# Layer 3 attention: the loads of a tile split by batch around the row transfers, the statistics two quads later, and one maximum over two neighbouring banks

## The reference

```
qh = q.reshape(B, h, dq, Lq)      # B 64, h 8, dq 8, Lq 256
kh = k.reshape(B, h, dq, Lk)      # Lk 256
qk = jnp.einsum('bhdq,bhdl->bhql', qh, kh) * scale
sm = jax.nn.softmax(qk, axis=-1)
ret = jnp.einsum('bhql,bhdl->bhdq', sm, vh)
return gamma * ret                # added to x
```

## Time and profile before

| | |
|---|---|
| median of 3 runs | 2188.28 us (2182.26 to 2192.83) |
| the profiled execution | 2183.03 us |
| its span, first to last instruction | 2181.2 us |
| layer 3 attention, first scores to last read | about 1419 to 1826 us of the span |
| PE busy, whole span | 1794.5 us (82%) |
| DVE busy, whole span | 1546.7 us (71%) |
| mean granted clock of PE | 0.919 |

### The profile page before, as it was taken

The page is one execution under the profiler, slowest core; times in us unless marked ns, Lnnn a source line. Parts: engine busy times, 40 slices in busy tenths (PEclk is TensorE's granted clock), DMA queues, the critical chain, the costliest instruction groups (busy, mean ns, idle before and its releaser), DMA issues. The chain is left out here.

```text
span 2181.2 us, 43555 instructions
## 1 busy us (share of the span) xinstructions
PE 1794.5 (82%) x14590; PEld 1355.5 (62%) x14590; DVE 1546.7 (71%) x3825; ACT 982.8 (45%) x2422; POOL 893.5 (41%) x1043
## 2 busy tenths in 40 slices
PE   6989846299796688988988789779888886989993
PEld 5879712188565577777777678744444442557772
DVE  7975741278649789889889666588888894654446
ACT  3743231035233445545544333347877785533330
POOL 3410016534238466666666520013443443643330
PEclk9989955699899799999999899979999998999996
DMA  7821036520214000000000211026777763433337
GB/s 227 295 81 59 11 98 184 160 73 6 71 34 127 1 0 0 0 0 0 0 0 1 59 30 31 1 54 140 157 140 146 145 137 92 122 108 100 108 105 246
DMA packets 150753, 182.46 MB, mean 84 GB/s; under 512 B 40193, under 2 KB 132593, under 8 KB 146481
## 3 DMA queue, kind: packets, MB, share of 16 engines
q1 hardware_dynamic: 140769, 158.05, 27.9%
q0 software_dynamic: 9808, 22.23, 3.4%
HBM read 121.78 MB, written 56.79 MB: 82 GB/s over the span
## 5 line engine op out<-in xcount | busy, mean ns | idle before, releaser
L2885 DVE TENSOR_REDUCE mx<-bank 128x2 f32<-128x512 f32 x512 | 315.8, 680 | 25.5 <-PE bank L2764 24.9
L2857 ACT ACTIVATE e<-bank 128x512 f32<-128x512 f32 x512 | 280.4, 598 | 90.7 <-PE bank L2786 86.2
L1914 POOL TENSOR_TENSOR q_l<-q_l,rot_l 64x512 f32<-64x512 f32 x128 | 162.3, 1268 | 129.6 <-DVE rot_l L2112 129.6
L2801 PE MATMUL bank<-e,val 128*32 128x256 f32 x2048 | 166.0, 396 | 8.9 <-ACT nd L2852 8.3
L2786 PEld LDWEIGHTS bank<-q,k 64*128 64x128 f32 x1024 | 78.6, 189 | 135.8 <-ACT e L2857 79.5
L2786 PE MATMUL bank<-q,k 64*128 64x256 f32 x1024 | 131.3, 335 | 26.2 <-DMA q<-rows 19.8
L2764 PE MATMUL bank<-k,q 62*128 62x256 f32 x1024 | 112.5, 299 | 23.7 <-DVE mx L2885 19.9
L1946 PE MATMUL bank<-qcT,wq_abs 96*128 96x128 f32 x1024 | 126.0, 283 | 0.0
L1946 PEld LDWEIGHTS bank<-qcT,wq_abs 96*128 96x128 f32 x1024 | 120.2, 196 | 2.6
L3072 POOL DMA_INDIRECT y<-y,y_row x71 | 69.0, 972 | 125.4 <-DVE y L3347 121.2
L1971 PE MATMUL bank<-wvo,rd_l 128*128 128x256 f32 x512 | 116.2, 380 | 0.0
(11 more groups left out here) (445 smaller groups left out, 4688.3 us busy)
## 6 DMA issues: line engine op xcount, KB each, us to landing
k<-k_parts SPq DMA_DIRECT2D x128, 128.0 KB, 5.2
q<-q_parts SPq DMA_DIRECT2D x64, 256.0 KB, 4.3
got<-rows SPq DMA_DIRECT2D x71, 129.0 KB, 2.1
k_parts<-k_parts_a SPq DMA_DIRECT2D x64, 128.0 KB, 3.3
moe_rows<-zero_a SPq DMA_DIRECT2D x16, 512.0 KB
w<-in_e0w SPq DMA_DIRECT2D x16, 512.0 KB, 3.7
q_parts<-parts SPq DMA_DIRECT2D x64, 128.0 KB, 2.7
rec<-rec_rows SPq DMA_DIRECT2D x64, 128.0 KB, 2.5
```

Source lines behind the costliest of these rows:

```text
L1914: nc.gpsimd.tensor_tensor(q[64:P, j, four(m), :], q[64:P, j, four(m), :], rot[64:P, j, four(m), :], ALU.add).then_inc(s["rope_added"], 1)
L2801: last = nc.tensor.matmul(readout[32 * g:32 * g + 32, side], val[:, a.n % 2, g, i, lt, :], e[:, slot(i, r), lt, :], start=(i == 0 and lt = ...
L2857: nc.scalar.activation(e[:, slot(i, r), :, :].rearrange("p k n -> p (k n)"), scoresT(i, r)[:, :], ACT.Exp).then_inc(s["exp_ready"], 1)
L2885: v.tensor_reduce(mx[:, a.n, r % 2, 0, at:at + 2], scores(r)[:, :].rearrange("p (a n) -> p a n", a=2), AX.X, ALU.max, negate=True).then_in ...
```

## The change

The change has three parts. The first is the order of SP's queue. `load` is cut by batch. Before, SP's `tile(a)` ended with all six loads of tile a+4; now `tile(a)` begins with the three loads of batch 0 of tile a+3, then comes `gather`, then `lay_rows`, then `store_inverse`, and only then the three loads of batch 1 and the values of tile a+3, `store` and `load_inverse`. The wait of the load for the freed buffer is the same (`turned_ready` of the last unit of tile a-1). The second is one reduction on DVE over two neighbouring banks in the place of two; for this the eight bank tensors become one tensor `banks` of which `bank[k]` is a slice. The third is where DVE does its small work: `norm` after pair 0 of quad 0, `invert` after pair 1 of quad 0 (before in quad 1), and `stats` after quad 2 (before after quad 1). PE, ACT and POOL keep their code.

```
-            def load(a):
-                sp.wait_ge(s[stored[a.n % 2]], 32 * (uses(a) + 1))
-                settle(sp, s["sp_passed"])
-                for b, base in enumerate(BASE3):
-                    q_rows = batch_rows(c.q_parts, a.t, b).unsqueeze(1)
...
+            def load(a, b):
+                if b == 0:
+                    sp.wait_ge(s["turned_ready"], unit_ready(a.t - BUF, 3, 3))
+                    sp.wait_ge(s[stored[a.n % 2]], 32 * (uses(a) + 1))
+                    settle(sp, s["sp_passed"])
+                base, q_rows = BASE3[b], batch_rows(c.q_parts, a.t, b).unsqueeze(1)
...
+            def load_values(a):
                 if a.exists(-BUF):
                     sp.wait_ge(s["val_ready"], tile_ready(a.t) - BUF)
...
             def tile(a):
+                loading = a.exists(-1) and a.exists(BUF - 1)
+                if loading:
+                    load(a.to(BUF - 1), 0)
+                if a.exists(-1):
+                    gather(a.to(-1))
                 if a.exists(1):
                     lay_rows(a.to(1))
                 if a.exists(-2):
                     store_inverse(a.to(-2))
+                if loading:
+                    load(a.to(BUF - 1), 1)
+                    load_values(a.to(BUF - 1))
                 if a.exists(AHEAD):
                     store(a.to(AHEAD))
-                if a.exists(-1):
-                    gather(a.to(-1))
                 if a.exists(-2):
                     load_inverse(a.to(-2))
-                if a.exists(BUF):
-                    sp.wait_ge(s["turned_ready"], unit_ready(a.t, 3, 3))
-                    settle(sp, s["sp_passed"])
-                    load(a.to(BUF))
...
-            def maxima(a, i, r):
-                if i == 0 and r == 0:
+            def maxima(a, i, p):
+                if i == 0 and p == 0:
...
-                dve.wait_ge(s["scores_ready"], unit_ready(a.t, i, r))
-                at = 2 * (QU * (r // 2) + i)
-                v.tensor_reduce(mx[:, a.n, r % 2, 0, at:at + 2], scores(r)[:, :].rearrange("p (a n) -> p a n", a=2), AX.X,
-                                ALU.max, negate=True).then_inc(s["max_ready"], 1)
+                dve.wait_ge(s["scores_ready"], unit_ready(a.t, i, 2 * p + 1))
+                at = 2 * (QU * p + i)
+                v.tensor_reduce(mx[:, a.n, :, 0, at:at + 2], c.banks[:, 2 * p:2 * p + 2, :].rearrange("p g (a n) -> p g a n", a=2),
+                                AX.X, ALU.max, negate=True).then_inc(s["max_ready"], 2)
...
+                        if (i, p) == (0, 0) and a.exists(AHEAD):
+                            norm(a.to(AHEAD))
+                        if (i, p) == (0, 1) and a.exists(-2):
                             invert(a.to(-2))
-                        if (i, r) == (1, 3) and a.exists(-3):
+                        if (i, p) == (2, 1) and a.exists(-3):
                             stats(a.to(-3))
```

More of the change, by code:

```diff
@@ L2599, in store @@
                                  whole(parts[:, a.n % 2, n, :])).then_inc(s[stored[a.n % 2]], 16)
-            def load(a):
-                sp.wait_ge(s[stored[a.n % 2]], 32 * (uses(a) + 1))
-                settle(sp, s["sp_passed"])
-                for b, base in enumerate(BASE3):
-                    q_rows = batch_rows(c.q_parts, a.t, b).unsqueeze(1)
[L2606 to L2610, removed]
+            def load(a, b):
[4 more added lines that the diff above has]
+                base, q_rows = BASE3[b], batch_rows(c.q_parts, a.t, b).unsqueeze(1)
+                sp.dma_start(whole(q[base:base + R, a.n, :]),
+                             q_rows.broadcast_to([2 * DQ3, 2, H3 * D])).then_inc(s[qk_loaded[a.n]], 16)
+                for m in range(2):
+                    sp.dma_start(whole(k[base + 2 * DQ3 * m:base + 2 * DQ3 * (m + 1), a.n, :]),
+                                 batch_rows(c.k_parts, a.t, b)).then_inc(s[qk_loaded[a.n]], 16)
+            def load_values(a):
                 if a.exists(-BUF):
@@ L2904, in tile @@
                 for i in range(QU):
-                    for r in range(4):
+                    for p in range(2):
                         if a.exists(LEAD):
-                            maxima(a.to(LEAD), i, r)
-                        if (i, r) == (1, 1) and a.exists(-2):
+                            maxima(a.to(LEAD), i, p)
+                        if (i, p) == (0, 0) and a.exists(AHEAD):
+                            norm(a.to(AHEAD))
+                        if (i, p) == (0, 1) and a.exists(-2):
                             invert(a.to(-2))
-                        if (i, r) == (1, 3) and a.exists(-3):
+                        if (i, p) == (2, 1) and a.exists(-3):
                             stats(a.to(-3))
-                        if (i, r) == (0, 2) and a.exists(AHEAD):
-                            norm(a.to(AHEAD))
             sch = Chain(dve, s["stat_chain"])
@@ L2917, in _ @@
                 for i in range(QU):
-                    for r in range(4):
-                        maxima(At(0, n), i, r)
+                    for p in range(2):
+                        maxima(At(0, n), i, p)
             finish_stats(nc, c, sch, LATE4)
@@ L3467, in build_program @@
         sb = lambda n, sh, dt=F32: ctx.enter_context(nc.sbuf_tensor(n, sh, dt))
-        c.bank = [ctx.enter_context(nc.psum_tensor(f"bank{k}", [P, 512], F32)) for k in range(8)]
+        c.banks = ctx.enter_context(nc.psum_tensor("banks", [P, 8, 512], F32))
+        c.bank = [c.banks[:, k, :] for k in range(8)]
         c.x = sb("x_all", [P, NT, D])
```

## The result

| | before | after |
|---|---|---|
| median | 2185.57 us (2182.26 to 2192.83, 4 runs) | 2291.31 us (2284.84 to 2299.5, 4 runs) |
| the profiled execution | 2183.03 us | 2284.84 us |
| its span | 2181.2 us | 2283.1 us |
| mean granted clock of PE | 0.919 | 0.889 |
| turned pairs, tile to tile, mean of tiles 2 to 29 | 12.07 us | 15.82 us |

The ratio is 1.048, 95% interval 1.0436 to 1.0526. The last row is worked out from the trace's starts of `turned_pair(a, 0, 0)` as in the earlier trace rows, here over the 28 tiles in which PE wants a tile that was loaded in the stage. Tile 1, which wants a tile loaded by the stage before, still lasts 11.01 us. The 28 tiles give 28 x (15.82 - 12.07) = 105 us more, what is ahead of tile 2 gives 1.6 us less and what is behind tile 29 1.5 us less, together the 101.9 us between the two spans.

What follows compares the result with a forecast made beforehand. Bound taken: waits between engines, then PE waiting for batch 1. 11.02 + 2.2 = 13.3, + 1.1 clock = 14.4 us a tile against 12.06, + 65.5 over 28 tiles; together + 63 on 2183.0: 2246, stated 2250 us; range about 2205 to 2283.

Steps and rivals of the forecast that it cites:

- The row wait: PE waiting for the row transfer q<-rows, 33.0 us on weight loads and 19.8 on matmuls; claimed gone after the change.
- the statistics wait: DVE waiting 31.1 us before the statistics for POOL's new x; claimed gone with the statistics four pairs after invert.
- The two-bank reduction: DVE's maximum: eight of about 1220 ns replace sixteen of 680 ns, 9.8 against 10.9 us a tile; claimed not to delay PE.
- the scores ahead of tile 0: Scores paced by DVE before tile 0: 16 pairs save at most 0.14 us each, 2.2 us.
- the loop: Closed path from score pair over rows, SP and load back to score pair; 11.02 + 2.2 = 13.3 us for each of 28 tiles.
- I take 5.1, nearer the lone ones, since only small transfers are in front of them: Batch 1's landing after its first issue: 5.1 us, between 4.84 and 5.94, so PE stands 2.2 us.
- the bound 5.94: Batch 1's landing if its last key load, issued at 1.14, takes 4.8 us as in the crowded queue.
- I take the smaller loss, 1.1 us, as the mean, because not every pause will do it: Time lost per tile to PE's clock falling to half after its pause: 1.1 us, bounds 0 and 2.4.
- a bigger clock loss, or a crowded load: Rival: load takes 5.94, PE stands 3.1 us, clock adds 1.4; 15.5 us a tile, + 96 us, 2283 us; chance 0.15.
- The tiles without a load: Tiles behind the last loaded one save what is left there of the 1.04 us a tile, put at 0.5.
- about 1.04 us a tile, 29 us in all, is what an ideal repair of both waits could return: Attention stage: tile 1 without PE's row wait or DVE's statistics wait lasts 11.02 us, tiles 1 to 28 12.06 each.
- The price by the Trainium skill: Batch 1's 512 KB at 2.0 us plus bytes over 436 GB/s: 3.2 us, PE stands 0.3 us, gain some 20 us.

Runs made afterwards that it cites:

- The best order found here: Against the kernel with load_inverse between the load's batches: POOL's finish behind the low part and q_parts store, DVE's statistics later; 2189.88 us, 0.9941 of before.
- the late queries: The full change with batch 1's two key loads issued at the head, only its 256 KB query load left behind row transfer and store_inverse: 1.0059 of before.
- both batches at the head: The full change with batch 1 of the load also issued at the head of SP's period, before gather and the row transfer: 0.9998 of before.
- the kernel with the filled round trip: Against the kernel with both batches at the head and q_parts stores on POOL: load_inverse moved between the two batches of the load; 1.0459 of before.

## Why the prediction was wrong in size

**What held.** The row wait and the statistics wait are gone in the changed kernel. PE waits instead for k<-k_parts at the first score pair, 28 times, and does not catch up. The two-bank reduction takes 1221 ns, against 1220 taken, and what lies ahead of tile 2 became 1.6 us shorter, against 2.2 for the scores ahead of tile 0. The rows go out 0.09 us after their cast and batch 1 2.93 us after the rows (3.04 taken), means over the tiles in which both occur. The order of the queue alone made the whole slowdown, so the loop is shown and not only argued.

**The first step that failed: "I take 5.1, nearer the lone ones, since only small transfers are in front of them".** Batch 1 landed 5.87 us after its first issue (mean; 5.85 median), next to the bound 5.94 that I worked out from the crowded queue. The reason given does not bear on it: with `store_inverse` taken away from in front of the load the landing was 5.82. Nor do the small transfers that are issued behind it explain much: batch 0 of the same kernel, behind which nothing is issued for some 1.7 us, took 5.67. The size that I had wrong is that of the last key load. I gave it 5.1 - 1.14 = 3.96 us from its own issue, near the 3.7 of a lone load; it was issued after 1.36 us and took 4.51, and only without the 256 KB of its own batch in front of it did it take 3.43. Why loads of one group slow each other, no run here tells. The first score pair came 2.9 us late instead of 2.2, so that the loop without any clock loss is 13.9 us a tile, where I had 13.3. The kernels with extra matmuls measure it at 14.0 and 14.15.

**The second: "I take the smaller loss, 1.1 us, as the mean, because not every pause will do it".** Every one of the 28 tiles had a stretch at the lower clock. From first to fourth turned pair a tile took 8.80 us in the mean, 4.75 more than tile 1; 2.89 of that is the late score pair, and the other 1.9 us are clock. By the length of a tile the kernels with extra matmuls give 1.67 and 1.8 us. Both pauses in the earlier trace rows had been followed by a fall, and I discounted that. The two terms together, 0.7 us of loop (2.9 against 2.2) and 0.7 of clock (1.8 against 1.1), are the 15.82 - 14.4 = 1.4 us a tile that were missing, some 40 us in all. This is the rival "a bigger clock loss, or a crowded load", which had 15.5 us a tile, and it was both.

**The tiles without a load** are not a term that failed. I counted tiles 1 to 28 as those that pause; they are 2 to 29, also 28, and what is behind tile 29 saved 1.5 us where I had 0.5.

**A step that the result hides: "about 1.04 us a tile, 29 us in all, is what an ideal repair of both waits could return".** The pace of 11.02 us exists: tile 1 runs at it before and after. But the two waits are not two sums to be won one by one. The repaired statistics wait went whole into the row wait, and the row wait goes only while a part of the load stands behind the rows, which closes the loop. With the megabyte back in front of them the rows land just behind it again, by the traces, as I had read it; what I had not read is that the load itself starts some 2 us late, since SP's queue is nearly full (10.2 us of issue in 12.1). The best order found here won 0.63 us a tile, 17.6 us by the tiles of its trace; the measured medians are 12.6 us apart.

**The price by the Trainium skill.** "DMA: Bandwidth & Descriptors", section "Anatomy of one DMA", gave an estimate of 3.2 us for 512 KB taken as one transfer, by a fit for the other descriptor path. The chip took 5.85, and for the 256 KB of the late queries 3.68, where the same form gives an estimate of 2.6 us. For these loads into few partitions the measurement decides, and a fit taken as a forecast would have told a gain.

## What to carry to other kernels

Before a transfer is moved behind another, follow what its consumer then releases: if that leads back to the transfer's own issue, the path is a loop, and once it is longer than the iteration was, its full length is the period of every iteration, with no slack to absorb an error; an experiment here fell into the same trap a second time through another engine. Price a transfer by the time from first issue to last landing of a group of its own size in its own traffic, not by a lone one, and if it makes TensorE pause, price the clock in every iteration until a row shows otherwise. A queue that only issues DMAs can be full: add its issue times and its round trips up like an engine's, since a wait repaired elsewhere goes into it.

## What was not expected of the hardware

- The time of a load followed its bytes much more than its count of DMAs: 256 KB late as one DMA or as two landed in 3.68 and 3.88 us and gave tiles of 12.50 and 12.51 us. 512 KB landed 2.2 us later than 256 KB (5.85 against 3.68), an estimate of some 120 KB a microsecond for the bytes added.
- A small transfer issued behind a large load seems to land with it: PE's pairs that waited for the rows started 0.7 to 1.1 us after the last landing of the load in seven kernels, while the time from the rows' own issue went from 4.4 to 5.9 us.
- The lower clock came in every tile of the changed kernel, over pauses of PE of 2.7 us in the mean, for 5.6 us of each tile, and not once in 28 tiles where 38 matmuls had cut the pause to 0.5 us in the mean (1.1 at most). The length of the pause alone does not tell it: over pauses of 1.4 us with 20 matmuls in front of them it came in 14 of 28 tiles, over bare pauses of 1.2 us (batch 1 ahead of `store_inverse`) in 24.
- SP's issue of a DMA is not a constant: two key loads took 1.04 us in most tiles and 2.29 in one shown; two of `load_inverse` 1.21 or 2.38. What stretches them was not tried.
- The same store of q_parts, issued by SP, landed in 2.4 us with both batches at the head and in 3.9 us in the changed kernel, where it is issued right behind batch 1 (medians); issued by POOL, in the kernel with the filled round trip, in 2.3. So it is the traffic around the store, more than the queue that issues it, that goes with the time.
